# Residual chain of four conditional layers on one core: another opening, with the identity turned by PE first, lora_B in 2 KB pieces, the scales loaded as 8 rows and turned by PE, and the thresholds sorted later

## The reference

```python
# layer 0: out = x @ W0.T + b0 + (x @ (2*mask - 1)) * coeff
# layer 1 (weight 1024 x 1024, lora_B 1024 x 64, lora_A 64 x 1024, groups of 128 columns):
lora_delta = lora_B @ lora_A * 0.5
cb = codebook / max(max(abs(codebook)), 1e-8)          # 8 levels
scale = exp(scale_log)                                 # 1024 rows x 8 groups
normalized = (weight + lora_delta) / scale
thresholds = (cb[:-1] + cb[1:]) * 0.5                  # 7 thresholds
quantized = cb[searchsorted(thresholds, normalized)]
w_eff = quantized * scale + lora_delta                 # value of the straight-through form
x = x + x @ w_eff.T
# layer 2: x @ W2.T + b2 + 2 * (x @ A[slot]) @ B[slot];  layer 3: (x @ B[id].T) @ A[id].T
```

## Time and profile before

| | us |
|---|---|
| median of 3 runs | 549.89 (549.53 to 550.72) |
| the profiled execution | 549.87 |
| its span, from the first to the last instruction | 548.2 |
| busy in the span: PE | 533.4 (97%) |
| busy: DVE | 468.8 (86%) |
| busy: ACT | 341.7 (62%) |
| busy: POOL | 192.9 (35%) |

### The profile page before, as it was taken

The page is one execution under the profiler, slowest core; times in us unless marked ns, Lnnn a source line. Parts: engine busy times, 40 slices in busy tenths (PEclk is TensorE's granted clock), DMA queues, the critical chain, the costliest instruction groups (busy, mean ns, idle before and its releaser), DMA issues.

```text
span 548.2 us, 8917 instructions
## 1 busy us (share of the span) xinstructions
PE 533.4 (97%) x2856; PEld 454.1 (83%) x2856; DVE 468.8 (86%) x723; ACT 341.7 (62%) x658; POOL 192.9 (35%) x179
## 2 busy tenths in 40 slices
PE   5999999999999999999999999999999999999997
PEld 4988888888888787887888788788888878878886
DVE  5998898988865879977999989998997998999862
ACT  3777776776745874586566657557566665755720
POOL 2669867987734020012034204111410420411130
PEclk9999999999999999999999999999999999999999
DMA  8766041843486995558456545645835654664122
GB/s 232 244 92 148 21 125 48 248 138 115 102 186 189 348 326 100 189 157 171 138 161 167 123 160 175 114 155 189 172 134 168 167 126 158 180 103 168 61 59 77
DMA packets 145261, 84.06 MB, mean 153 GB/s; under 512 B 102672, under 2 KB 118032, under 8 KB 145104
## 3 DMA queue, kind: packets, MB, share of 16 engines
q1 hardware_dynamic: 143312, 78.97, 52.4%
q0 software_dynamic: 1632, 4.72, 3.4%
q10 hardware_dynamic: 288, 0.01, 0.0%
HBM read 67.43 MB, written 16.25 MB: 153 GB/s over the span
## 4 chain that ended last, share of the span: by engine, by line
PE 83%; DVE 9%; ACT 4%; DMA 3%; issue 1%; POOL 0%; DVEq 0%; ACTq 0%; SPq 0%; POOLq 0%
PE bank L1637 19%; PE bank L1644 10%; PE bank L1676 7%; PE bank L1677 7%; PE bank L1675 7%; PE bank L1511 5%; PE bank L1513 5%; PE bank L1512 5%; PE bank L1726 3%; PE bank L1725 3%; PE bank L1727 3%; PE bank L1691 3%; PE bank L1421 2%; PE bank L1704 1%; DVE w_lo L1074 1%; DVE merged_ring L1168 1%
## 5 line engine op out<-in xcount | busy, mean ns | idle before, releaser
L1637 PE MATMUL bank<-x_t_pair,m_hi 128*128 128x512 f32 x512 | 128.5, 393 | 1.5 <-ACT m_hi L800 1.4
L800 ACT CAST m_hi<-merged_ring 128x512 fp32r<-128x512 f32 x128 | 73.1, 619 | 60.7 <-PE bank L1644 31.9
L1637 PEld LDWEIGHTS bank<-x_t_pair,m_hi 128*128 128x128 f32 x512 | 92.5, 189 | 19.2 <-ACT m_hi L800 2.3
L1174 DVE TENSOR_TENSOR m_lo<-merged_ring,m_hi 128x512 fp32r<-128x512 f32 x128 | 86.3, 720 | 12.5 <-ACT m_hi L800 12.2
L576 POOL TENSOR_TENSOR x_t_pair<-x_sum,x_t_pair 128x256 fp32r<-128x256 f32 x32 | 29.7, 960 | 179.1 <-ACT x_t_pair L861 179.1
L1168 DVE TENSOR_TENSOR merged_ring<-merged_ring,w_t 128x1024 f32<-128x1024 f32 x64 | 82.1, 1311 | 11.3 <-ACT merged_ring L790 10.3
L790 ACT ACTIVATE merged_ring<-mask_ring,batch_now 128x1024 f32<-128x1024 int32 x64 | 78.0, 1241 | 21.1 <-DMA mask_ring<-in_mask_Bx4096x_ik 20.3
L1644 PEld LDWEIGHTS bank<-x_t_pair,m_lo 128*128 128x128 f32 x512 | 69.8, 190 | 5.0
L1644 PE MATMUL bank<-x_t_pair,m_lo 128*128 128x256 f32 x512 | 71.4, 282 | 0.0
L1676 PE MATMUL bank<-P_lo,x_t_pair 128*128 128x512 f32 x160 | 62.3, 389 | 0.0
L1675 PE MATMUL bank<-P_hi,x_t_pair 128*128 128x512 f32 x160 | 62.3, 389 | 0.0
(11 more groups left out here) (211 smaller groups left out, 1133.5 us busy)
## 6 DMA issues: line engine op xcount, KB each, us to landing
mask_ring<-in_mask_Bx4096x_ik SPq DMA_DIRECT2D x64, 512.0 KB, 4.4
w_nat<-in_L_cond_W SPq DMA_DIRECT2D x14, 512.0 KB, 5.3
x_t_squares<-in_x SPq DMA_DIRECT2D x56, 128.0 KB, 3.0
w_raw<-in_L_cond_weight SPq DMA_DIRECT2D x16, 256.0 KB
out<-out_staged SPq DMA_DIRECT2D x16, 256.0 KB, 4.5
w0t_dram<-w_out SPq DMA_DIRECT2D x14, 256.0 KB, 2.6
g_batch<-g_dram POOLq DMA_DIRECT2D x28, 128.0 KB, 4.3
w_t<-w0t_dram SPq DMA_DIRECT2D x6, 512.0 KB, 5.1
```

The costliest lines, as they stand in the source:

```text
L800: nc.scalar.copy(Mh[:, n % MR], ring_f[:, k % MR, h * HALF:(h + 1) * HALF]).then_inc(s["h_set"], 1)
L1174: nc.vector.tensor_tensor(Ml[:, n % MR], ring_f[:, k % MR, h * HALF:(h + 1) * HALF], Mh[:, n % MR].bitcast(F32), ALU.subtract).then_inc(s[ ...
L1637: mm(bank[L0_BANK[HT * h + j]][:, :], Mh[:, n % MR, j * P:(j + 1) * P], xThl[:, :, :, k + i, :], start=(k + i == 0), stop=False, skip_grou ...
```

## The change

- PE: as soon as the identity is made, 14 turns of the identity into bank 0 (nobody reads them), then lora_B, then eight small turns that bring the exponentiated scales from 8 partitions to 128, into bank 2.
- lora_B is loaded with eight neighbouring rows to a partition, one piece of 2 KB, where it had eight pieces of 256 B. The turned rows are then in another order, and ACT's copy spreads them (a step of 8 elements in the destination).
- The scales are loaded as 8 rows of 4 KB in place of 1024 pieces of 32 B, second in SP's list. ACT takes the exponential there (8 partitions by 1024, read with a step of 8 elements), ahead of the lora_B copies. DVE takes the reciprocal from the bank, and a copy of the scales.
- The codebook load moves from SP's list to ACT's, behind the tokens.
- DVE sorts the thresholds after `add_delta(0)`, where it did so before it (11 instructions, from the steps `dd` on, with all their code unchanged).
- PE's list has `w2_transpose(1)` before the two `b3_transpose`; ACT's has `w2_hi(1)` and `mid_up(0)` before the two `b3_set`.

```diff
@@ sync @@
-            sp.dma_start(lbn[:, :, :], lora_b.rearrange("(t p) r -> p t r", p=P)).then_inc(s["lora_b_in"], 16)
+            sp.dma_start(lbn[:, :, :], lora_b.rearrange("(p t) r -> p t r", t=KT)).then_inc(s["lora_b_in"], 16)
+            sp.dma_start(scn[:, :], scale_log.rearrange("(t p) g o -> t (p g o)", p=P)).then_inc(s["sc_in"], 16)
             sp.dma_start(la[0:RL, :], lora_a).then_inc(s["lora_a_in"], 16)
-            sp.dma_start(cb[:, :], row(codebook).broadcast_to([P, NCB])).then_inc(s["cb_in"], 16)
-            sp.dma_start(sc[:, :, :], scale_log.rearrange("(t p) g o -> p t (g o)", p=P)).then_inc(s["sc_in"], 16)
@@ scalar @@
+            act.dma_start(cb[:, :], codebook.rearrange("(o n) -> o n", o=1).broadcast_to([P, NCB])).then_inc(s["cb_in"], 16)
...
+            act.wait_ge(s["sc_in"], 16)
+            nc.scalar.activation(sce[:, :, :], scn[:, :].rearrange("t (p g) -> t g p", g=G), ACT.Exp).then_inc(s["scale_set"], 1)
             for h in range(2):
                 act.wait_ge(s["lbt_tr"], h + 1)
-                nc.scalar.mul(lbt[0:RL, h * 512:(h + 1) * 512], bank[5 + h][0:RL, :], L1_SCALE).then_inc(s["lbt_set"], 1)
-            act.wait_ge(s["sc_in"], 16)
-            nc.scalar.activation(sc[:, :, :], sc[:, :, :], ACT.Exp).then_inc(s["scale_set"], 1)
-            act.wait_ge(s["scale_set"], 1)
+                spread = lbt[0:RL, :].rearrange("r (p t) -> r t p", t=KT)[:, h * HT:(h + 1) * HT]
+                nc.scalar.mul(spread, bank[5 + h][0:RL, :].rearrange("r (t p) -> r t p", p=P), L1_SCALE).then_inc(s["lbt_set"], 1)
             norm(0)
             w2_hi(0)
             inner_up(0)
+            w2_hi(1)
+            mid_up(0)
             b3_set(0)
             b3_set(1)
-            w2_hi(1)
-            mid_up(0)
             w2_hi(2)
@@ vector @@
-            dve.wait_ge(s["scale_set"], 1)
-            nc.vector.reciprocal(rs[:, :, :], sc[:, :, :]).then_inc(s["recip_set"], 1)
-            step.did(nc.vector.tensor_tensor(dd[:, :], cb[:, 1:NCB], cb[:, 0:NTH], ALU.subtract))
...
+            dve.wait_ge(s["scale_turned"], 1)
+            scale_bank = bank[2][:, 0:G * KT].rearrange("p (g t) -> p g t", t=KT)
+            nc.vector.reciprocal(rs[:, :, :], scale_bank).then_inc(s["recip_set"], 1)
+            nc.vector.tensor_copy(sc[:, :, :], scale_bank).then_inc(s["scale_placed"], 1)
...
             add_delta(0)
+            step.did(nc.vector.tensor_tensor(dd[:, :], cb[:, 1:NCB], cb[:, 0:NTH], ALU.subtract))
...
+            dve.wait_ge(s["scale_placed"], 1)
             nc.vector.tensor_scalar(cs[:, :, :], sc[:, :, :], cb[:, 0:1], None, ALU.mult).then_inc(s["first_level"], 1)
             add_delta(1)
@@ tensor @@
             pe.wait_ge(s["ident_set"], 1)
+            for _i in range(WARM):
+                nc.tensor.transpose(bank[0][:, 0:P], ident[:, :], ident[:, :])
             pe.wait_ge(s["lora_b_in"], 16)
...
+            pe.wait_ge(s["scale_set"], 1)
+            for g in range(G):
+                ins = nc.tensor.transpose(bank[2][:, g * KT:(g + 1) * KT], sce[:, g], ident[0:KT, 0:KT])
+            ins.then_inc(s["scale_turned"], 1)
...
             w2_transpose(0)
+            w2_transpose(1)
             b3_transpose(0)
             b3_transpose(1)
-            w2_transpose(1)
             v_part(0)
```

More of the change, by code:

```diff
@@ L210, in cond_resid_chain @@
             ub_in b2row_in x_in0 x_in1 g_in recip_set first_level tok_in b2c_in b2col_set numbers_set rows_set ident_set ident_zero own_set ub_zero
[L211 removed]
+            scale_turned scale_placed lbt_tr lbt_set w2_tr w2_hi w2_lo b3_tr b3_set b2_tr b2_set v_done v_hi v_lo bb_done a3_tr a3_set ga_done ab_hi ab_lo b3b2_set y_set gsum_set scale_set cb_set coef_set ga_hi ga_lo
             delta_done raw_used w2_eyed eff_plain normed terms pool_added scaled inner_set inner_up mid_set mid_up eff_set w1_hi_set w1_ready
@@ L622, in scaled @@
                     blk, k = pooled[:, h, t * P:(t + 1) * P], h * HT + t
-                    nc.scalar.activation(blk, blk, ACT.Identity, bias=cs[:, k, q:q + 1], scale=sc[:, k, q:q + 1]).then_inc(s["scaled"], 1)
+                    nc.scalar.activation(blk, blk, ACT.Identity, bias=cs[:, q, k:k + 1], scale=sc[:, q, k:k + 1]).then_inc(s["scaled"], 1)
             def norm(n):
@@ L633, in norm @@
                 for t in range(HT):
-                    nc.scalar.activation(bank[NORM][:, t * P:(t + 1) * P], raw[:, h, t], ACT.Copy, scale=rs[:, h * HT + t, q:q + 1]).then_inc(s["normed"], 1)
+                    nc.scalar.activation(bank[NORM][:, t * P:(t + 1) * P], raw[:, h, t], ACT.Copy, scale=rs[:, q, h * HT + t:h * HT + t + 1]).then_inc(s["normed"], 1)
             def inner_up(n):
@@ L1457, in b3_transpose @@
                     pe.wait_ge(s["b3_in"], 16)
+                else:
+                    pe.wait_ge(s["scale_placed"], 1)
                 for t in range(HT):
```

34 lines of the change are left out of this document (18 added, 16 removed).

## The result

The changed kernel has a median of 552.69 us (552.02 to 554.00, 6 runs), beside 550.54 (549.53 to 550.77, 6 runs) for the kernel before in the same session: a ratio of 1.0046, 95% interval 1.0032 to 1.0059. By the ratio it is slower by 2.5 us (1.8 to 3.2); 550.4 was forecast, with 548.7 to 551.9 as the range. The profiled execution has 552.48, 2.61 above that of before, and a span of 550.8.

A forecast was written before the change was run, and what follows sets the result against it. PE, busy for 481.42 of 483.00 us from 62 us on, was taken as the bound, so only the opening counts. Head -1.15 plus tail +1.7 gives +0.55 on 549.87: 550.4 us, range 548.7 to 551.9.

The forecast's parts named there:

- The head: Opening up to DVE's first comparison: to gain 1.15 us, bounds 0.35 to 2.2.
- F: Start of DVE's first comparison: forecast at 12.0, 13.14 in the kernel before.
- its sign of being wrong: DVE's first comparison before 10.9 or after 12.8, or DVE finding `w2_hi(2)` ready.
- The tail: Behind DVE's first comparison: the reordering, with both `b3_set` behind `mid_up(0)`, costs 1.7 us, bounds 1.6 to 2.6.
- PE up to the lora_B turns: PE's opening: 14 slow identity turns from 1.75 to 4.85, lora_B landed at 3.9, its eight turns done at 6.45.
- the 6.8 that I took: PE's opening: time at which its clock rises to full speed, the middle between 4.85 and 8.75.
- `delta(0)` is then PE's from 7.6 to 8.55.: PE, behind the scale turns: eight passes of 0.12 at full speed, result ready at 8.75.
- The step of 8 elements: ACT's exponential and lora_B copies: no new cost; at twice the price, `delta(0)` 0.2 later than DVE asks.
- If it still lands for 7.92 the part ends at 9.17: DVE's codebook part in the opening, 1.25 long: ends at 9.17, 8.35 or 7.3 to 7.85; 8.35 taken.
- S: Start of the second half group's first comparison on DVE: 23.95 in place of 21.91, 2.0 late, in the old clock.
- 29.85 for `w2_lo(4)`: DVE in the tail: `w2_lo(4)` at 29.85 where it was at 28.2, in the old clock.
- No head gain: Rival in the opening: codebook as late as now or late clock, -0.35 + 1.7 gives 551.2; chance 0.15.

The follow-up runs named there:

- e6: Kernel before with only the new PE and ACT order, plus 18 unread identity turns before `v_part(0)`: 552.32 us, ratio 1.0033.
- e2: Kernel before with only the new PE and ACT order, its opening unchanged: 553.22 us, ratio 1.0052.
- e8: Changed kernel with the step of 8 elements moved from ACT's exponential to the weights PE loads for the scale turns: 552.80 us, ratio 1.0045.
- e10: Changed kernel with the old PE and ACT order behind the opening, lora_A loaded in two pieces, the second behind the raw weights: 552.22 us, ratio 1.0031.
- e1: Changed kernel with the old PE and ACT order behind the opening, the rest of the change kept: 550.21 us, ratio 0.9982.
- e5: Changed kernel with the old PE and ACT order behind the opening, and the scales' exponential taken after PE's turn: 550.58 us, ratio 1.0006.
- e4: Changed kernel with PE turning the raw scales and ACT taking the exponential from the bank behind the lora_B copies: 553.05 us, ratio 1.0037.
- e7: Changed kernel, new order kept, with 11 more identity turns by PE ahead of `delta(0)`: 555.40 us, ratio 1.0097.
- e9: Changed kernel with the old PE and ACT order behind the opening and 11 more identity turns ahead of `delta(0)`: 552.20 us, ratio 1.0017.
- e12: Changed kernel with the old PE and ACT order, exponential after the turn, lora_A in two pieces, 8 identity turns ahead of `delta(0)`: 553.83 us, ratio 1.0049.
- e11: Changed kernel with the old PE and ACT order behind the opening and without the 14 starting identity turns: 551.18 us, ratio 0.9994.

## Why the prediction was wrong

Two terms of its sum failed. The head was to gain 1.15, with DVE's first comparison at 12.0: `delta(0)` was taken to start at 7.6 and started at 8.74, and F was 13.73, beyond the 12.8 that the prediction itself had set as its sign of being wrong. The tail was to cost 1.7, which it does where the clock stays up (1.8 in e6); over all executions the order costs 2.9 (e2), and e2's rows and granted clocks show PE's clock falling in the pause that the order makes. By its own steps:

- **PE up to the lora_B turns.** Right: turns from 1.72 (1.75), lora_B in time, its turns from 4.76 (4.9). That lora_B landed at 4.5, not 3.9, was hidden behind the 14 turns; the row that 3.9 was taken from is a store, not a load. The clock rose during them (1.39 for eight), earlier than the 6.8 that I took; the scale turns cost 0.66, less than the 1.15 that was taken.
- **"`delta(0)` is then PE's from 7.6 to 8.55."** This is the step that failed. It started at 8.74 and its 8 passes took about 1.8. Three things are in it:
  - The landing of lora_A was never asked for. It was issued behind lora_B and the scales, 0.36 later than in the kernel before, took 6.8 where it had taken 6.2, and landed at 8.65. e8 and e10 show each cause alone: without the exponential's step it is lora_A (8.09), without lora_A it is ACT (8.34).
  - The step of 8 elements was priced by "up to 0.2 later". It was taken at the old price for the exponential (up to 1.5) and at nothing for the copies; it costs 2.05 - 1.06 = 1.0 and 2 x 0.4. The bound was also added up wrongly: from 6.45, two copies at twice 0.59 end at 8.8, not at 8.1; they ended at 8.60. The rule of the Trainium skill that I had quoted (SBUF — State Buffer, Door 1: The DMA port swizzle) was the right warning, and e8's pair of rows is the trace that agrees with it; the page gives no factor, the rows give 1.9.
  - Between, PE stood for 0.59 and 1.34, and the clock that I let rise once and stay fell again: about 0.8 for `delta(0)`.
- **DVE.** "If it still lands for 7.92 the part ends at 9.17": it ended at 8.46 here, so the value taken (8.35) was good; but in other executions the codebook came at 8.4 (e1) and 9.14 (e5). In these three it was hidden behind `delta(0)`. Where `delta(0)` ran at full speed it was not: in e4, e7, e9 and e12 the codebook came at 7.64 to 8.47, and `add_delta(0)` started at 9.58 to 10.28 right behind DVE's own work, without a wait. So once `delta(0)` was out of the way the codebook was the next to hold the head. The sorting between the two `add_delta` took 12.97 - 11.36 = 1.61 where 1.34 was costed; one instruction of it has 0.37, beside an identity add of POOL.
- **The head**: +0.59 in place of -1.15 in this pair of traces, outside its bounds (a gain of 0.35 to 2.2). That it loses is not shown, since the old opening alone had F from 13.03 to 13.76. That the forecast gain did not come is: in the six traces with this exponential and these copies and the scales issued second (changed, e1, e7, e9, e10, e11) F was 13.00 to 13.95, and in none of the experiments was it below 12.35. By the ratios the head with the old order gains 1.0 us (0.1 to 1.9) in e1 and 0.3 (-0.4 to 1.0) in e11.
- **The tail**: 1.67 for 1.7 in the profiled execution, its stations within 0.1 counted from F, but for S, which was 0.17 earlier than forecast (10.64 behind F for 10.81). The last one, 29.85 for `w2_lo(4)`, was set down without its sum; in the same count it was 29.80. What it left out is what the same pause does to the clock. In the changed kernel's trace the clock had fallen before it and was up again for `v_part(0)`; where it was up before (e2, e4), it fell in it and cost 1.6 more, and e6, with the pause filled, has neither. So the 0.03 between 1.67 and 1.7 is in part the luck of the profiled execution. That 3.5 us come back in the ratios when the order is undone, and 1.9 in the traces, would fit such falls in the other executions of the changed kernel; no trace of them shows it.
- **The chances.** "No head gain" was a rival at 551.2; it was too mild, since it let the head gain its lower bound still. A head that loses was not among the cases.

What stays open: 0.37 of the 2.61, which lies behind the sixteenth half group's first comparison, where traces differ by up to 1.9 anyway; what the new head is worth over many executions; why an S that is 0.74 earlier (e8) is not seen in the time; and what decides, in one execution, whether the clock falls in a pause of 1.2 to 2.3.
